# A gate multiplied into the finished row on ScalarE, two turns behind VectorE, in a mixture-of-experts loop

## What is computed

```python
for e in range(E):
    h = jax.nn.relu(xf @ w1[e] + b1[e]) @ w2[e] + b2[e]
    y = _layernorm(xf + h, gamma[e], beta[e])
    w = jnp.sum(jnp.where(idx == e, gates, 0.0), axis=-1)
    out = out + w[:, None] * y
```

## Time and profile before

| what | us |
|---|---|
| median of 3 runs | 952.72 (947.23 to 955.12) |
| the profiled execution | 951.93 |
| its span, first to last instruction | 950.2 |
| the experts' loop, from the first transpose to the last scatter | 554.2 to 904.4 |
| reading back and summing, behind it | to 950.2 |

### The profile page before, as it was taken

One profiled execution on the slowest core, in us unless ns is written; L12 is line 12 of the kernel. 1 busy time (PEld: TensorE's weight loads), 2 busy tenths in 40 slices (PEclk: granted clock), 3 DMA queues, 4 the chain that ended last, 5 costly groups with the idle time before them and its releaser, 6 DMA issues.

```text
span 950.2 us, 27864 instructions
## 1 busy us (share of the span) xinstructions
PE 803.2 (85%) x7821; PEld 677.0 (71%) x7822; DVE 771.8 (81%) x3156; ACT 570.0 (60%) x1536; POOL 500.9 (53%) x660
## 2 busy tenths in 40 slices
PE   1799998979999999999997289999999998999600
PEld 1599998956777777777776168888888898888500
DVE  1768788635889999999997638999999999999956
ACT  2633351037899999999996336666666666566400
POOL 3000000000478888887887726777777777777700
PEclk9999999989999999999996589999999999999855
DMA  8444230080112121212122354222222222222089
GB/s 168 119 80 85 59 60 1 1 244 14 41 53 61 55 63 56 60 55 58 56 61 66 85 196 161 69 75 72 72 65 75 73 69 66 69 76 75 25 315 389
DMA packets 68202, 84.19 MB, mean 89 GB/s; under 512 B 12067, under 2 KB 52694, under 8 KB 67978
## 3 DMA queue, kind: packets, MB, share of 16 engines
q1 hardware_dynamic: 52295, 53.27, 20.4%
q0 software_dynamic: 12256, 22.50, 7.6%
q10 hardware_dynamic: 3555, 7.23, 2.3%
HBM read 48.15 MB, written 35.71 MB: 88 GB/s over the span
## 4 chain that ended last, share of the span: by engine, by line
PE 57%; DVE 18%; issue 9%; DMA 8%; ACT 3%; SPq 2%; POOL 2%; DVEq 1%; ACTq 1%; POOLq 0%
PE ps L676 8%; PE ps L935 7%; PE ps L776 5%; DVE arena L1045 4%; DMA arena<-y_tokens 4%; PE ps L751 3%; PE ps L762 3%; PE ps L811 3%; PE ps L924 3%; PE ps L830 3%; PE ps L825 3%; PE ps L757 2%; DVE arena L1369 2%; PE ps L844 2%; PE ps L926 2%
## 5 line engine op out<-in xcount | busy, mean ns | idle before, releaser
L587 POOL DMA_INDIRECT y_tokens<-arena x184 | 183.1, 995 | 90.8 <-DVE arena L1390 50.9
L560 POOL DMA_INDIRECT x_slots<-arena x192 | 190.5, 992 | 58.1 <-POOL arena L558 44.8
L935 PE MATMUL ps<-arena 128*128 x1472 | 180.7, 276 | 0.1
L935 PEld LDWEIGHTS ps<-arena 128*128 128x128 f32 x1472 | 171.5, 192 | 1.8 <-issue 0.8
L1628 ACT ACTIVATE arena<-ps,b_t 128x256 f32<-128x256 f32 x368 | 144.2, 474 | 22.1 <-issue 15.0
L676 PE MATMUL ps<-wt,arena 128*128 128x128 f32 x960 | 118.0, 280 | 12.0 <-DVE arena L1045 12.0
L676 PEld LDWEIGHTS ps<-wt,arena 128*128 128x128 f32 x960 | 112.7, 195 | 13.4 <-DVE arena L1045 13.4
L924 PE MATMUL ps<-arena 128*128 128x256 f16 x368 | 101.5, 276 | 17.2 <-DVE arena L1338 13.2
L925 PE MATMUL ps<-arena 128*128 128x256 f16 x368 | 100.9, 274 | 0.0
L926 PE MATMUL ps<-arena 128*128 128x256 f16 x368 | 100.8, 274 | 0.0
L565 POOL MEMSET arena<- 128x258 f32 x1 | 0.3, 317 | 190.4 <-DVE arena L1293 190.4
(11 more groups left out here) (208 smaller groups left out, 1815.4 us busy)
## 6 DMA issues: line engine op xcount, KB each, us to landing
arena<-x_slots SPq DMA_DIRECT2D x92, 130.0 KB, 2.2
arena<-y_tokens SPq DMA_DIRECT2D x17, 640.0 KB, 14.2
h<-h_rows SPq DMA_DIRECT2D x1, 5440.0 KB, 17.0
out<-h ACTq DMA_DIRECT2D x17, 320.0 KB, 9.1
arena<-x_in SPq DMA_DIRECT2D x64, 84.5 KB
arena<-x_in SPq DMA_DIRECT2D x56, 78.0 KB
h_rows<-h SPq DMA_DIRECT2D x32, 128.0 KB
x_slots<-arena POOLq DMA_INDIRECT x192
```

What stands on the lines that cost most here:

```text
L560: pool.indirect_dma_start(xs_dram, bass.IndirectOffsetOnAxis(ap=slot_i[n][0:rows, t, k:k + 1], axis=0), row[n][0:rows, k, t, :], None).the ...
L587: pool.indirect_dma_start(y_dram, bass.IndirectOffsetOnAxis(ap=y_id[n % 2][:, k:k + 1], axis=0), y_sl[n % 2][:, k, :], None, bounds_check= ...
L935: ins = pe.matmul(ps[6 + m][:, 128 * k:128 * k + 128], hid[m][:, c, 128 * k:128 * k + 128], w2_sb[:, bass.ds(e, 1), c, :].rearrange("p o n ...
```

## The change

The gate leaves the norm: `gated_rstd` is gone, and `tile_norm` waits for `tile_rstd` and multiplies by 1/std alone. `shifted` adds beta to both halves in one instruction of 256 columns and writes a new tile `z` (two buffers). A new step `gated_rows` on ScalarE, of tile i-6, multiplies each half of `z` by the gate, with the gate as a pointer scale, into `y_sl`; it stands between `upper_half` and `tile_rstd`. `y_first` and `y_ready` are set by its two activations. `scatter_y` moves from tile i-5 to tile i-6 and waits for both. `shifted` waits, after the row numbers, until tile i-2 has left its `z`. The pipeline has one turn more at its end.

```diff
-LAST_TILE_LAG = 5
+LAST_TILE_LAG = 6
...
+        z = [A3.take(2, E_DIM) for _ in range(2)]
...
             def scatter_y(i, n, u, e):
+                pool.wait_ge(S["y_first"], i + 1)
                 pool.wait_ge(S["y_ready"], i + 1)
...
                 at(2, with_bias)
-                at(5, scatter_y)
+                at(6, scatter_y)
...
-            def gated_rstd(i, n, u, e):
+            def tile_norm(i, n, u, e):
                 dve.wait_ge(S["rstd3_ready"], i + 1)
-                dve.tensor_tensor(rg3, rstd3, x_sl[n][:, :, E_DIM], ALU.mult).then_inc(S["gate_ready"], 1)
-
-            def tile_norm(i, n, u, e):
-                dve.wait_ge(S["gate_ready"], i + 1)
                 need(dve, S["scl_ready"], i)
                 for k in range(2):
-                    ins = dve.tensor_scalar(nrm[:, k, :], res[n % 2][:, k, :], mv3[:, k, 0:1], rg3[:, k:k + 1],
+                    ins = dve.tensor_scalar(nrm[:, k, :], res[n % 2][:, k, :], mv3[:, k, 0:1], rstd3[:, k:k + 1],
                                             ALU.subtract, ALU.mult)
...
             def scaled(i, n, u, e):
                 dve.wait_ge(S["norm_ready"], i + 1)
-                need(dve, S["y_ready"], i)
+                need(dve, S["z_ready"], i)
...
                 need(dve, y_gone[n % 2], 32 * (XBUF // 2 * u + n // 2))
                 ch.step(dve.tensor_copy(y_id[n % 2], x_sl[n][:, :, E_DIM + 1]))
-                be = bet_all[:, bass.ds(e, 1), :].rearrange("p o n -> p (o n)")
-                for k in range(2):
-                    ins = dve.scalar_tensor_tensor(y_sl[n % 2][:, k, :], be, g[:, k:k + 1], scl[:, k, :],
-                                                   ALU.mult, ALU.add)
-                    if k == 0:
-                        ch.step(ins)
-                ins.then_inc(S["y_ready"], 1)
+                need(dve, S["y_ready"], i - 1)
+                be = bet_all[:, bass.ds(e, 1), :].to_broadcast([128, 2, E_DIM])
+                dve.tensor_tensor(z[n % 2], scl, be, ALU.add).then_inc(S["z_ready"], 1)
...
                 at(2, sums)
-                at(3, gated_rstd)
...
             def tile_rstd(i, n, u, e):
                 act.wait_ge(S["rstd3_stats"], i + 1)
-                need(act, S["gate_ready"], i)
+                need(act, S["norm_ready"], i)
...
+            def gated_rows(i, n, u, e):
+                act.wait_ge(S["z_ready"], i + 1)
+                act.activation(y_sl[n % 2][:, 0, :], z[n % 2][:, 0, :], ACT.Copy, scale=x_sl[n][:, 0, E_DIM:E_DIM + 1])\
+                   .then_inc(S["y_first"], 1)
+                act.activation(y_sl[n % 2][:, 1, :], z[n % 2][:, 1, :], ACT.Copy, scale=x_sl[n][:, 1, E_DIM:E_DIM + 1])\
+                   .then_inc(S["y_ready"], 1)
...
                 at(0, upper_half)
+                at(6, gated_rows)
                 at(4, tile_rstd)
...
-DVE_TILE = 5
+DVE_TILE = 4
```

More of the change, by code:

```diff
@@ L296, in build @@
         nrm, scl = A3.take(2, E_DIM), A3.take(2, E_DIM)
+        z = [A3.take(2, E_DIM) for _ in range(2)]
         y_sl = [A3.take(2, E_DIM) for _ in range(2)]
-        bns3, mv3, ln3, rstd3, rg3 = (A3.take(2, 6), A3.take(2, 2), A3.take(2), A3.take(2), A3.take(2))
+        bns3, mv3, ln3, rstd3 = A3.take(2, 6), A3.take(2, 2), A3.take(2), A3.take(2)
         y_id = [A3.take(2, dt=I32) for _ in range(2)]
@@ L319, in build @@
             "cnt_ready cnt_ps tab_f_ready tab_ps pad_first pad_ready tab_ready pad_gone pad_stored xs0 "
-            "xs1 xs2 xs3 xs4 xs5 xs6 xs7 norm_ready scl_ready gate_ready bns3_ready xt_ps xhi_ready xlo_ready "
+            "xs1 xs2 xs3 xs4 xs5 xs6 xs7 norm_ready scl_ready z_ready y_first bns3_ready xt_ps xhi_ready xlo_ready "
             "h_ps h_ready w2_ps xb_ready t_ready rstd3_stats rstd3_ready y_ready yg0 yg1 yl0 yl1 yl2 yl3 "
@@ L1381, in shifted @@
             def shifted(i, n, u, e):
-                g = x_sl[n][:, :, E_DIM]
                 dve.wait_ge(S["scl_ready"], i + 1)
```

## The result

Measured side by side, four runs each:

| | before | after |
|---|---|---|
| median, us | 951.43 (947.23 to 955.12) | 963.23 (960.98 to 966.1) |
| the profiled execution | 951.93 | 966.1 |
| its span | 950.2 | 964.3 |
| first transpose of the loop | 554.2 | 558.0 |
| first hidden matmul of the first tile to that of the last | 332.7 | 340.3 |

A forecast was written before the change was run, and what follows sets the result against it. VectorE, with what GpSimd holds up, was taken to set the pace, TensorE 0.36 us a turn behind. 951.9 + 3 (loop, 84 turns) + 1 (end) = 956 us; own range 945 to 962, for 8 in 10 937 to 968.

The forecast's parts named there:

- The round: Expert loop: moments, rstd, relu, upper half, gate, scatters, landing, row numbers, back to moments; 9.96 us per three turns unblocked.
- The rival A: Expert loop: the round has slack and TensorE sets the pace, 27.1 to 27.8 for eight turns, 932 us; chance 0.26.
- pattern of three, two short and one long: Sign in the expert loop that the forecast is right: two turns of 3.3 us and one near 4.
- 29.7: Eight turns of the expert loop after the change, in us: 28.0 plus 1.7 of register reads, against 29.4 before.
- the register reads: Reads of eight expert registers once in eight turns: ScalarE 1.55, VectorE 1.6; 1.05 to 3.15 in the round, taken 1.7.
- scaled: VectorE step in the round, 0.39 us, expected to meet GpSimd's add: 0 to 0.8 us a round, taken 0.5.
- 0.7 stays: VectorE's hold-ups by GpSimd remain 0.7 us a turn after the change, giving 26.9 us for eight turns.
- VectorE's relief: Two steps fewer and one new add shorten VectorE's turn from 2.75 to 2.46; eight turns 26.9, 2.5 less.
- VectorE near 85% busy: Sign that the forecast is right: VectorE's busy share in 600 to 880 us of the changed kernel.
- throughput sum for the loop: By throughputs alone TensorE would set the expert loop: 26.6 plus 0.5 to 1.2 for its register read, 27.1 to 27.8.
- Rival B: Start of each block of eight turns: register reads fall on the round entirely, 31.2 for eight, 971 us; chance 0.26.
- The end: After the loop: the last tiles' scatters come later, behind gated_rows, in two such steps; +1 to +2 us, taken +1.

The follow-up runs named there:

- gate_first_no_bias: The kernel after with gated_rows at the head of ScalarE's turn and without GpSimd's add of b2: 1025.64 us, ratio to before 1.0101.
- the second session: Kernels before and after run again, each with and without GpSimd's add of b2, at full TensorE clock: 948.71, 962.19, 924.15 and 945.81 us.
- no_bias: The kernel after without GpSimd's add of the bias b2: 945.81 us, ratio to before 0.9929, 80 tiles in 284.4.
- dve_only_again: The kernel before with VectorE's two edits alone, gate left out: 1003.26 us, ratio to before 0.9939; in the first session 1031.02 us.
- gate_first: The kernel after with gated_rows at the head of ScalarE's turn: 1030.99 us, ratio to before 0.9994; run again 999.62 us, ratio 0.9834.
- before_no_bias: The kernel before without GpSimd's add of the bias b2: 924.15 us, ratio to before 0.9706, 80 tiles in 267.1.
- the second pair: The kernels before and after, unchanged, run once more on one chip: 948.71 and 962.19 us.
- after_again: The kernel after, unchanged, run once more: 962.19 us, ratio to before 1.0107, 80 tiles in 301.2.
- before_again: The kernel before, unchanged, run once more: 948.71 us, ratio 1.0001, 80 tiles in 285.5.

## Why the prediction was right, and where its sizes were off

**The round: right, and shown.** "All this closes a round that is not in the kernel before" holds. L1384 waits 39.2 us in the stretch instead of 1.4; without GpSimd's add the new order costs 17.3 us over 80 tiles by itself; and two edits that break it in different places, one by position and one by buffers, both remove the wait nearly or wholly and leave a shorter loop, in their two sessions and against the 301.2 of the others. That nothing else keeps the loop from TensorE's pace is not shown: `gate_first_no_bias` lacks the round and the add and did not reach it. The rival A (TensorE sets the pace) fell: 3.77 a turn is 0.45 above its 3.32. One sign did not come: the turns have no pattern of three, two short and one long. From one start of L1360, the moments, to the next, eight turns in a row go 2.5, 4.8, 3.7, 2.9, 3.7, 4.0, 4.8, 3.7.

**Its terms.** From the gate's start at 705.73 to its end at 706.44 it is 0.71 (forecast 0.67); from there to the scatter 0.85 (0.86); to the second one 1.30 (1.31). These terms of the round are right to a few hundredths. Eight turns take 30.1 us (8 x 280 / 74.4) against "29.7", and the second session tells which term was under-sized. In `no_bias` no add can hold anything up, and the 1.77 over the round's 9.96 is what the prediction took for the register reads (1.7). With the add eight turns grow from 28.3 to 30.1, that is 0.7 a round, where the prediction took 0.5, for the meeting of "scaled" with GpSimd's add alone. The hold-ups are the mis-sized term, as far as this pair tells (it takes GpSimd's work away with them). The groups of all norms and gamma steps in the kernel after, 600 to 880, show where they fell:

```profile
L1367 DVE TENSOR_SCALAR arena<-arena 128x128 f32<-128x128 f32 x148 | 69.3, 512 | 0.0
L1377 DVE TENSOR_TENSOR arena<-arena 128x256 f32<-128x256 f32 x74 | 39.1, 528 | 0.0
L1387 DVE TENSOR_TENSOR arena<-arena 128x256 f32<-128x256 f32 x75 | 32.0, 426 | 0.4
```

and the same two steps of the kernel before:

```profile
L1369 DVE TENSOR_SCALAR arena<-arena 128x128 f32<-128x128 f32 x152 | 45.9, 343 | 0.0
L1379 DVE TENSOR_TENSOR arena<-arena 128x256 f32<-128x256 f32 x76 | 32.4, 427 | 0.0
```

The norm grew from 343 to 512 ns apiece and the gamma step from 427 to 528, both inside the round, where before the waiting fell on L1363 and L1390, which are gone. The pair of norms is busy 0.94 us a turn (69.3 / 74) against 0.60 (45.9 / 76); the round counted it with nothing in its way, 0.51 from its start to the next step's, and put the whole hold-up on "scaled". The hold-ups did not vanish with the two steps; they moved to the next ones that share a moment with GpSimd.

**The price of the hold-ups.** The prediction weighed 0.63 by the rule of the Trainium skill (SBUF — State Buffer, "Who interferes with whom") against "0.7 stays". The pair of runs without the add prices them: VectorE is busy 244.92 / 73.2 = 3.35 a turn before and 224.95 / 78 = 2.88 without the add, 0.47; in the new order 3.06 and 2.64, 0.42. The ratio of 0.42 to 0.47 is that of 0.63 to 0.7, but both are smaller than either forecast, and the difference is too small to decide between them. On one point the traces speak against the Trainium skill's "exclusive lock", read as one instruction after the other: GpSimd's add at 704.78 keeps its 0.72 while L1377, begun in the same moment, ends only 0.28 after it, where one after the other would give 0.40.

**VectorE's relief.** "VectorE near 85% busy" came out at 82%. Forecast was that the relief of 2.5 us in eight turns buys nothing, because the round takes its place. `dve_only_again`, the relief without the round, bought 0.6% (interval 0.2 to 1.1%), and its turn of 3.62 is far above both TensorE's 3.32 and VectorE's forecast 26.9 / 8 = 3.36. So the prediction's throughput sum for the loop (27.1 to 27.8) would have been wrong even without the round. What is in the way there is not settled. `gate_first`, with the same relief, the round cured and more work on ScalarE, is 5.7 and 8.2 us shorter than `dve_only` over the 80 tiles in the two sessions, so the later scatter can even be worth something; no run here separates that. GpSimd is the candidate: its turn of 3.18 and register read give 3.4, its add taken out brings the kernel before to 3.33. But that edit takes GpSimd's work and the hold-ups away together, and these runs do not separate them.

**ScalarE.** Right: 214.21 / 74.4 = 2.88 us a turn (forecast 2.9), hidden as throughput, as `gate_first` shows with the same instructions in a faster loop. The pair's groups:

```profile
L1632 ACT ACTIVATE arena<-arena 128x128 f32<-128x128 f32 x74 | 31.5, 425 | 0.3 <-DVE arena L1387 0.2
...
L1634 ACT ACTIVATE arena<-arena 128x128 f32<-128x128 f32 x74 | 31.2, 421 | 0.0
```

Each is 0.42 where I took 0.40. The prediction also weighed a rule of the Trainium skill (ScalarE: Activation LUTs, "Rules for kernel authors") that would keep multiplies on VectorE. The runs support neither side of it as a matter of speed: with the multiplication on ScalarE `gate_first_again` has the fastest loop that kept all of the work (279.2), and the kernel after the slowest (301.2). Between these two only the place in the queue differs.

**Register reads.** Rival B would have had all 3.15 us of them in the round and 971 us. The 1.77 of `no_bias`, which also holds whatever else its round costs over 9.96, speaks against it. TensorE's read, taken as 0.5 to 1.2, costs next to nothing: before_no_bias runs 26.7 us for eight turns against 26.6 without any read.

**The end.** +1 was forecast and +3.0 came (from the last hidden matmul to the last tile's scatter 14.4 to 17.5, and 14.5 to 16.8 in the second pair). The last turns of the kernel after, in the timeline:

```profile
904.11 0.46 DVE L1384 CAST arena<-arena 128x2 int32<-128x2 f32 x1 [2.99 <-DMA y_tokens<-arena]
...
912.41 0.17 DVE L1384 CAST arena<-arena 128x2 int32<-128x2 f32 x1 [0.33 <-DMA y_tokens<-arena]
...
915.40 0.17 DVE L1384 CAST arena<-arena 128x2 int32<-128x2 f32 x1 [1.32 <-DMA y_tokens<-arena]
916.01 0.40 ACT L1632 ACTIVATE arena<-arena 128x128 f32<-128x128 f32 x1 [2.30 <-DVE arena L1387]
...
917.54 0.98 POOL L589 DMA_INDIRECT y_tokens<-arena  x1 [0.71 <-issue]
```

Even with the loop running empty four of the last five casts wait for the landing of the tile before last: the round goes on after the steady part. The prediction had counted two such steps, at +1 to +2, and took the lower end.

**Before the loop.** +3.8 us was in no step of the prediction. It is real: the first transpose comes at 558.0, 558.2 and 557.7 in after, after_again and no_bias, and at 554.2, 553.5 and 553.8 in the three kernels of the old order, though this part of the code is untouched. The windows view, 90 to 135, of the kernel before and of the kernel after:

```profile
90.00:135.00 45.00, 41.66 (x382) 41.27 (x382) 36.40 (x135) 16.21 (x24) 0.00 (x0) 1.00 0.38 75
```

```profile
90.00:135.00 45.00, 41.65 (x352) 41.26 (x352) 35.44 (x131) 15.71 (x22) 0.00 (x0) 0.92 0.40 74
```

TensorE was as busy ahead of it in the one as in the other (48.98 and 48.99 of the 54 us from 53). Eight of the nine traces of the new order show 0.92 to 0.96 in this stretch, `gate_first_no_bias` and the five of the old order 1.00; why the drop comes with the one order and not the other stays open. Some 3.8 of the 11.8 us between the medians are thus no effect of the experts' loop at all.

**How good the hit is.** The value missed by some 7 us: 3.8 before the loop, 4.6 in it (7.6 against 3), 2.0 at its end (3.0 against 1), less the 2.9 that the median lies below the profiled execution. All three parts erred the same way, and the number missed the forecast's own range by 1 us and stayed in the wide one. The starting point was lucky: had the prediction stood on before_again's execution (943.12, 80 tiles in 285.5), a loop of 29.7 for eight turns would have been 11.5 us slower over the 80 tiles, and the same reasoning would have forecast "slower". The pace of the new round was forecast; its difference to a loop that itself varies by 8 us was not something one profile could give.

## What to carry to other kernels

When a step moves to another engine's in-order queue, walk from the release of its buffer around to the next use of it, count the turns that lie between, and put into that round all that is queued ahead of the moved step: here 9.96 us over three turns, level with the busiest engine and so without slack. If the round is as long as the pace, put the moved step at the head of its turn or give the small buffer (here two words per partition) more copies before moving any work. And profile the kernel before more than once where engines meet by phase, since one execution's loop can lie 3% from another's.

## What the runs showed of the hardware

- The loop of one and the same kernel took 293.7 and 285.5 us for 80 tiles at full TensorE clock. VectorE is busy 3.51 us a turn in the one (267.06 / 76.1) and 3.35 in the other (244.92 / 73.2), with the same instructions, so it is held up less; without GpSimd's add the loop runs at 267.1, just TensorE's own pace.
- A VectorE step of 0.40 us that began in the same moment as a GpSimd add took 1.00, while the add kept its 0.72: the step is held up for most of the add, not for all of it.
- GpSimd takes 0.85 to 0.86 us from the end of the instruction that it waits for to the start of an indirect DMA, in both kernels.
- The granted clock fell to 0.92 over 90 to 135 us in one program and not in the other, whose instructions there are the same; and sessions differ in it, 0.94 over the span in one and 0.88 to 0.92 in two others, at 6 to 9% more time for the same kernel.
